# History product of a chunked recurrence: four heads side by side on TensorE, results through DRAM, no interleaving by hand

## The chip, the cores and the metric

The kernel runs on one core of a Trainium2 chip. The metric is the device time of one launch in microseconds; lower is better. The kernel before was timed three times: 3161.13, 3158.82 and 3152.03 us, median 3158.82 us.

## The reference, cut to what matters

The kernel is one decoder layer: a gated delta-rule attention, a long convolution and a mixture of experts, each followed by a layer norm. The change touches only the recurrence of the attention. For each of 16 sequences and 16 heads it is, over 128 time steps, with a state `S` of 128 x 128 in float32:

```
Sk = einsum('bhij,bhj->bhi', St, kt)
err = Sk - vt
Sn = at[..., None] * St - (bt[..., None] * err)[..., None] * kt[:, :, None, :]
ot = einsum('bhij,bhj->bhi', Sn, qt)
```

The state is never built. `S` at time t is a sum over earlier times r of a decayed vector u(r) times k(r), so `Sk` and `ot` are sums over r of u(r), scaled by the products k(r)·k(t) and k(r)·q(t), which an earlier stage put into a matrix `gram`.

## The kernel before, in words

`recurrence` puts 128 pairs (8 sequences x 16 heads) on the 128 partitions and calls that a group; there are two groups g. Time is cut into 8 chunks c of 16 steps. One (c, g) is a leaf, so there are 16 leaves, in the order (0,0), (0,1), (1,0) and so on. In the text below "round c" is a pair of leaves.

Inside a leaf VectorE walks the 16 steps (`leaf`, line 541 on). The second eight steps need sums over the first eight; part of them comes from TensorE: `cross_z` (line 771) for `Sk`, in five fills, and `cross_o` (line 797) for `ot`. Both multiply by diagonal matrices that ScalarE builds (`diagonal_z`, `diagonals_o`). VectorE adds the first fill of `cross_z` at line 627 at the start of the second half, and must have it there. TensorE may start `cross_z` of a leaf once VectorE has passed that leaf's first half (`half_done`) and `outputs` of the leaf before has read its bank (`o_seen`).

Everything older than the chunk is the history. At the end of leaf (c, g), for 0 < c < 7, VectorE multiplies all older rows in `hist[g]` by the chunk's decay, in pieces of 32 rows (line 664). SyncE stores the chunk's own 16 rows (lines 745 and 746) and then the decayed pieces (line 749) to `history` in DRAM, and loads them back turned, with the time rows on the partitions (line 762), beside the columns of `gram` (line 756). The turned rows of line 762 are loaded only when all stores have landed. One unit is four heads of one sequence; a leaf has 32 units in 8 buffers. For each head TensorE multiplies: stationary operand the turned rows (up to 112 x 128), moving operand 32 columns of `gram` (line 825). The result has the value index on the partitions. ScalarE copies it to `z_turn` (line 889), TensorE turns it back with 32 transposes per leaf (line 848), ScalarE copies those into `zo[g]` (line 915), and that is where leaf (c+1, g) starts from.

TensorE works in order. The units of the history product of leaf (c, g) are placed by hand with the table `ORDER`: some behind the last units of `cross_o` of the same leaf, 10 (rounds 0 to 2) or 8 (rounds 3 to 6) right behind `cross_o`, some between the units of `cross_z` of the following leaf, the rest behind it. GpSimd loads decays, `beta_v` and `gram` for later leaves and stores the outputs (`load_half`, `load_gram`, `store_o`).

Of the kernel before, what the change touches and what calls it, by code (L numbers as in the profile page):

```python
# [416 lines left out]
def recurrence(nc, a_dram, bv_dram, gram_dram, beta_dram, hist_dram, o_dram):  # L417
# [13 lines left out]
    HU = H // 4  # L431
    UB = H // HU
    UNITS = BG * UB
    NTURN = 8
# [9 lines left out]
    ORDER = ((0, 3, 12, 10, 4), (3, ROUNDS, 14, 8, 5))  # L444
    with ExitStack() as ctx:
# [14 lines left out]
        z_turn = m.sb("p2_z_turn", [DH, P, 2 * C])  # L460
        ident = m.sb("p2_ident", [P, P])
        NDZ, NDO = 2, 2
# [3 lines left out]
        ps_z = [m.ps(f"p2_ps_z{i}", [DH, H, 2 * C]) for i in range(2)]  # L466
        ps_t = [m.ps(f"p2_ps_t{i}", [P, 4, DH]) for i in range(2)]
# [33 lines left out]
        t_done = m.sem("p2_t_done")  # L501
        t_cp = m.sem("p2_t_cp")
        zo_ready = [m.sem(f"p2_zo_ready{g}") for g in range(GR)]
        TD = 2
        TB = 2 * C // 4
# [3 lines left out]
        with nc.Block() as start:  # L509
            @start.sync  # L510
            def _(sp):
                for sem in (*zo_ready, mm_done, z_cp, t_done, t_cp):
                    sp.sem_inc(sem, FREE)
                sp.sem_inc(diag_o_used, NDO)
# [22 lines left out]
        def _(dve):  # L537
# [3 lines left out]
            def leaf(c, g):  # L541
# [119 lines left out]
                if 0 < c < ROUNDS:  # L661
                    dve.wait_ge(kept[g], c * 2)
                    for r0, rows in pieces(c):
                        nc.vector.tensor_tensor(out=hist[g][:, r0:r0 + rows], in0=hist[g][:, r0:r0 + rows],
                                                in1=zo[g][:, 0, 0:1, :].broadcast_to([P, rows, DH]),
                                                op=ALU.mult).then_inc(hist_done[g], 1)
# [18 lines left out]
        def _(pool):  # L685
# [46 lines left out]
            for g in range(GR):  # L732
                pool.wait_ge(o_out[g], DMA * NCHUNK)


        @block.sync
        def _(sp):
            def by_seq(g, r0, n):
                return hist_dram[g, r0:r0 + n].rearrange("r p i -> p r i")

            for c in range(ROUNDS):
                rows, t1 = (c + 1) * C, (c + 1) * 2 * C
                for g in range(GR):
                    sp.wait_ge(leaf_done, c * GR + g + 1)
# [5 lines left out]
                    for u in range(UNITS):  # L750
                        n = g * UNITS + u
                        i = n % NTURN
                        b, h0 = u // UB, u % UB * HU
                        if c or n >= NTURN:
                            sp.wait_ge(mm_done, c * (GR * UNITS) + n - NTURN + 1 + FREE)
                        sp.dma_start(gcol[i][0:rows], gram_dram[g * BG + b, h0:h0 + HU, 0:rows, t1:t1 + 2 * C]
                                     .rearrange("h r e -> r h e")).then_inc(turned_in[i], DMA)
                        if u == 0:
                            sp.wait_ge(u_saved[g], (c + 1) * 2 * DMA)
                            if c:  # L760
                                sp.wait_ge(hist_saved[g], carried(c + 1) * DMA)
                        sp.dma_start(turned[i][0:rows], hist_dram[g, 0:rows, u * HU:(u + 1) * HU]).then_inc(turned_in[i], DMA)

        @block.tensor
        def _(pe):
            pe.wait_ge(cleared, 2 * NTURN + 2)

            def cross_z(c, g, between=lambda u: None):
# [6 lines left out]
                for j, (k0, k1) in enumerate(Z_FILLS):  # L775
                    if j == 4:
                        pe.wait_ge(x_z_read, c * (GR * len(Z_FILLS)) + g * len(Z_FILLS) + 1)
                    for k in range(k0, k1):
                        for q in range(2):
# [7 lines left out]
                            if not (k == k1 - 1 and q == 1):  # L787
                                between(u)
                    pe.wait_ge(diag_z_used, at + u)
                    pe.sem_inc(x_done, 1)  # L790
                    between(u)

            def cross_o(c, g, between=lambda u: None):
# [4 lines left out]
                for j, (k0, k1) in enumerate(O_FILLS):  # L798
                    for k in range(k0, k1):
                        for q in range(2):  # L800
# [7 lines left out]
                            between(u)  # L808
# [4 lines left out]
            for c0, c1, o_units, first, z_units in ORDER:  # L813
                with pe.Fori(c0, c1) as c:
                    for g in range(GR):
                        def history(u):

                            n = g * UNITS + u
                            i = n % NTURN
                            k = g * BG + u // UB  # L820
                            pe.wait_ge(turned_in[i], c * (GR * UNITS // NTURN * TD * DMA) + (n // NTURN + 1) * TD * DMA)

                            pe.wait_ge(z_cp, (c * (GR * BG) + k - 1 if k >= 2 else c * (GR * BG)) + FREE)
                            for h in range(HU):
                                last = nc.tensor.matmul(ps_z[k % 2][:, u % UB * HU + h, :], turned[i][:, h, :],  # L825
                                                        gcol[i][:, h, :], start=True, stop=True)
                            last.then_inc(mm_done, 1)

                        todo = list(range(UNITS))

                        def history_past(units):
                            def between(u):
                                if todo and u > units:
                                    history(todo.pop(0))
                            return between
# [19 lines left out]
        def _(act):  # L855
# [43 lines left out]
            for c in range(ROUNDS):  # L899
                rows_after = (2, 2, 2, 8, 12, 16, 16, 16) if c < 3 else (2, 2, 9, 13, 16, 16, 16, 16)  # L900
# [1070 lines left out]
```

## Time and profile before

| | us |
|---|---|
| median of three runs | 3158.82 |
| the profiled execution | 3169.36 |
| its span, first to last instruction | 3167.7 |
| first step of the recurrence on VectorE | 678.8 |
| last operation of the recurrence on VectorE ends | 2046.5 |
| VectorE busy, whole span | 2219.2 (70%) |
| TensorE matmuls busy, whole span | 2513.2 (79%) |
| mean granted TensorE clock | 0.821 of 2.4 GHz |

The recurrence takes 43% of the span. Times in rows are counted from the span's start. A busy share over the whole span mixes stages with different limits, so what a wait inside the recurrence costs has to be read inside it. TensorE has one record for the weight load (PEld) and one for the matmul (PE) of each pass; one float32 matmul of the kernel leaves two records of each.

### The profile page before, as it was taken

What the parts mean: (1) busy time and instruction counts of PE and PEld (TensorE: products, weight loads), DVE (VectorE), ACT (ScalarE), POOL (GpSimd) and SP (SyncE); (2) the same over time, 40 slices, a digit from 0 to 9 for tenths busy, and PEclk for the clock granted to TensorE, in tenths of its full rate; (3) what the DMA queues carried; (4) which work ended last, traced back from release to release, by engine and by line L of the source; (5) the groups of instructions that cost most, each with busy time, mean ns of one, the idle gap of its engine ahead of it and who ended that gap; (6) DMA issues with size and microseconds to landing.
All of it is one profiled execution on the core that took longest, in us unless ns stands there. A gap on an engine that the chain in (4) does not pass through costs nothing. (4 is left out here: it accounts for less than half of the span.)

```text
span 3167.7 us, 44608 instructions
## 1 busy us (share of the span) xinstructions
PE 2513.2 (79%) x12946; PEld 1944.7 (61%) x12946; DVE 2219.2 (70%) x5854; ACT 1250.0 (39%) x2980; POOL 773.2 (24%) x700
## 2 busy tenths in 40 slices
PE   8999999937989998989988888589968481389900
PEld 4555555526888888889887778478753250157700
DVE  5778778879888899898899987855527565013334
ACT  2555555524555555454555453532310010112200
POOL 1444344320000000000000000044435116501175
PEclk8999999967888888677877787899989665679955
DMA  2343434332233345655777775152230422029832
GB/s 95 119 125 118 123 121 122 118 110 69 73 84 92 106 130 137 160 148 149 193 206 203 209 190 152 37 163 73 76 107 20 133 98 74 6 83 267 245 100 87
DMA packets 488010, 389.69 MB, mean 123 GB/s; under 512 B 146255, under 2 KB 423550, under 8 KB 483336
## 3 DMA queue, kind: packets, MB, share of 16 engines
q1 hardware_dynamic: 440555, 285.62, 32.0%
q0 software_dynamic: 26784, 87.09, 9.0%
q10 hardware_dynamic: 20480, 14.69, 1.4%
q8 instruction: 89, 1.46, 0.2%
q14 instruction: 102, 0.84, 0.1%
HBM read 215.13 MB, written 178.41 MB: 124 GB/s over the span
## 5 line engine op out<-in xcount | busy, mean ns | idle before, releaser
L559 DVE SCALAR_TENSOR_TENSOR p_zo<-p_w,p_gd,p_zo 128x128 f32<-128x128 f32 x2304 | 649.0, 345 | 11.3
L825 PE MATMUL p_ps_z<-p_gcol,p_turned 112*128 112x32 f32 x3584 | 567.1, 322 | 55.9 <-DMA p_turned<-history 42.8
L825 PEld LDWEIGHTS p_ps_z<-p_gcol,p_turned 112*128 112x128 f32 x3584 | 560.8, 247 | 65.1 <-issue 37.4
L384 DVE SCALAR_TENSOR_TENSOR p_y<-p_ps_proj,p_w,p_y 128x508 f32<-128x508 f32 (+2 forms) x576 | 415.9, 741 | 114.0 <-ACT p_y L298 100.5
L804 PE MATMUL p_ps_x<-p_w,p_diag_o 128*128 128x128 f32 x2048 | 314.8, 305 | 69.0 <-ACT p_diag_o L866 45.5
L234 PE MATMUL p_ps_proj<-p_x,p_w 128*128 128x512 f32 x768 | 341.5, 594 | 2.7 <-ACT p_beta_t L289 2.7
L866 ACT ACTIVATE p_diag_o<-p_ident,p_gd 128x128 f32<-128x128 f32 x1024 | 316.7, 389 | 63.9 <-PE p_ps_x L804 55.2
L804 PEld LDWEIGHTS p_ps_x<-p_w,p_diag_o 128*128 128x128 f32 x2048 | 273.0, 209 | 106.3 <-ACT p_diag_o L866 65.1
L879 ACT ACTIVATE p_diag_z<-p_ident,p_gd 128x128 f32<-128x128 f32 x768 | 247.8, 390 | 212.4 <-PE p_ps_x L783 190.0
L783 PE MATMUL p_ps_x<-p_w,p_diag_z 128*128 128x128 f32 x1536 | 259.8, 317 | 61.2 <-DVEq L578 43.7
L783 PEld LDWEIGHTS p_ps_x<-p_w,p_diag_z 128*128 128x128 f32 x1536 | 221.3, 219 | 74.1 <-issue 50.9
L198 POOL TENSOR_TENSOR p_kq<-p_y,p_sig 128x512 f32<-128x512 f32 x128 | 162.5, 1274 | 376.3 <-ACT p_sig L309 375.7
L234 PEld LDWEIGHTS p_ps_proj<-p_x,p_w 128*128 128x128 f32 x768 | 141.6, 191 | 157.2 <-issue 153.9
L687 POOL DMA_DIRECT2D p_dec<-decays x32 | 17.3, 542 | 800.7 <-DVEq L660 738.7
L889 ACT COPY p_z_turn<-p_ps_z 128x512 f32<-128x512 f32 x112 | 64.7, 578 | 345.9 <-PE p_ps_z L825 345.9
L298 ACT ACTIVATE p_y<-p_ps_proj,p_w 128x512 f32<-128x512 f32 x192 | 149.3, 777 | 61.0 <-PE p_ps_proj L234 56.3
L556 DVE TENSOR_TENSOR p_w<-p_w,p_dec 128x256 f32<-128x256 f32 (+3 forms) x224 | 168.0, 750 | 0.5
L1086 PE MATMUL p_ps_g<-p_xT,p_wg 128*128 (+1 forms) x512 | 116.5, 387 | 33.8 <-DMA p_wg<-in_wgT 31.2
L256 PE MATMUL p_ps_gram<-p_kq 128*128 128x256 f32 x512 | 129.4, 396 | 4.6 <-POOL p_v L198 4.6
L1563 PE MATMUL p_ps_d<-p_sd,p_hs 88*128 88x256 f32 x128 | 58.7, 637 | 89.7 <-DVE p_hs L1685 49.2
L1086 PEld LDWEIGHTS p_ps_g<-p_xT,p_wg 128*128 128x128 f32 x512 | 98.3, 194 | 49.7 <-DMA p_wg<-in_wgT 31.4
L309 ACT ACTIVATE p_sig<-p_y 128x512 f32<-128x512 f32 x192 | 119.5, 623 | 4.5 <-issue 3.5
(213 smaller groups left out, 3600.3 us busy)
## 6 DMA issues: line engine op xcount, KB each, us to landing
history<-p_hist SPq DMA_DIRECT2D x18, 2048.0 KB, 10.8
gram<-p_gram SPq DMA_DIRECT2D x64, 512.0 KB, 3.3
p_wgu<-in_wguT SPq DMA_DIRECT2D x64, 352.0 KB
decays<-p_dec SPq DMA_DIRECT2D x64, 256.0 KB, 2.3
beta_v<-p_bv SPq DMA_DIRECT2D x64, 256.0 KB, 2.4
p_dec<-decays POOLq DMA_DIRECT2D x32, 512.0 KB, 6.4
p_w<-beta_v POOLq DMA_DIRECT2D x16, 1024.0 KB, 5.9
heads_out<-p_zo POOLq DMA_DIRECT2D x16, 1024.0 KB, 9.4
```

The lines of the kernel that those rows point to most:

```text
L198: nc.gpsimd.tensor_tensor(out=dst, in0=y[u % 4][:].rearrange("p (b t) -> p b t", b=QB), in1=sig[u % 2][:].rearrange("p (b t) -> p b t", b=QB),
L234: last = nc.tensor.matmul(ps_proj[u % 4][:], w_sb[j % 2][:, k, kind, :], x_sb[:, k, n * 512:(n + 1) * 512], start=(k == 0), stop=(k == KT ...
L298: nc.scalar.activation(y[u % 4][:], ps_proj[u % 4][:], ACT.Identity, bias=par[j % 2][:, kind, TAPS:TAPS + 1], scale=par[j % 2][:, kind, TA ...
L384: nc.vector.scalar_tensor_tensor(out=yv[:, :, s:], in0=pv[:, :, 0:T - s], scalar=par[j % 2][:, kind, TAPS - 1 - s:TAPS - s], in1=yv[:, :, ...
L556: return done(nc.vector.tensor_tensor(out=out, in0=in0, in1=in1, op=ALU.mult))
L559: return done(nc.vector.scalar_tensor_tensor(out=acc, in0=row, scalar=scalar, in1=acc, op0=ALU.mult, op1=ALU.add))
L783: last = nc.tensor.matmul(ps_x[:, j % 4, k - k0, :], diag_z[u % NDZ][:, e, :], w[g][:, 1 + r, :], start=(r == 0), stop=(r == RZ - 1))
L804: last = nc.tensor.matmul(ps_x[:, O_BANK + j, k - k0, :], diag_o[u % NDO][:, e, :], w[g][:, 1 + r, :], start=(r == 0), stop=(r == RO - 1))
L825: last = nc.tensor.matmul(ps_z[k % 2][:, u % UB * HU + h, :], turned[i][:, h, :], gcol[i][:, h, :], start=True, stop=True)
L866: last = nc.scalar.activation(diag_o[u % NDO][:, e, :], ident[:], ACT.Copy, scale=gd[g][:, r0 + e, C + HALF + k:C + HALF + k + 1])
L879: last = nc.scalar.activation(diag_z[u % NDZ][:, e, :], ident[:], ACT.Copy, scale=gd[g][:, r0 + e, HALF + k:HALF + k + 1])
L1086: last = nc.tensor.matmul(ps_g[g % 2][:, e, :], wg[:, k, (2 * g + e) * DH:(2 * g + e + 1) * DH], xT_sb[:, k, bass.ds(p * (PB * T), PB * T) ...
```

## The change

Stationary and moving operand change places. The stationary operand is now the 32 columns of `gram` of a head, the moving one its turned rows (128 columns), and four heads write to four groups of 32 partitions of one PSUM tile. The result has (head, column) on the partitions and the value index along the row. A unit is eight heads: 16 units per leaf, in 4 buffers of twice the size; the turned rows are loaded in pieces of 4 KB instead of 2 KB. `z_turn`, the 32 transposes and the copies of line 915 are gone. Instead ScalarE copies each sequence's result to `sums` and issues a DMA to a DRAM scratch `history_sums` (8 stores of 256 KB per leaf), and SyncE loads it into `zo[g]` in two halves of 1 MB.

`ORDER` and the interleaving are gone: TensorE does `cross_o`, then all 16 units, then `cross_z` of the following leaf. `gram` columns of the first four units are loaded ahead of the leaf's end. For those four units the chunk's own 16 rows are loaded once they have been stored, and the older rows once their stores have landed. Decay, store and load of the older rows stay at the end of the leaf. ScalarE has four buffers for `diag_z` instead of two: it makes four of the 16 `diag_z` units ahead of the eight copies of the history product, and twelve behind them.

```diff
-    HU = H // 4
+    HU = H // 2
-    NTURN = 8
+    NTURN = 4
+    QUADS = HU // 4
-    ORDER = ((0, 3, 12, 10, 4), (3, ROUNDS, 14, 8, 5))
+    NZ = 4
+    TL = 2 * (UNITS // NTURN) + 1
-        NDZ, NDO = 2, 2
+        NDZ, NDO = 4, 2
...
-                dve.wait_ge(zo_ready[g], c + FREE)
+                if c:
+                    dve.wait_ge(zo_in[g], c * (2 * DMA))
...
+            sp.wait_ge(cleared, 2 * NTURN + 2)
             for c in range(ROUNDS):
                 rows, t1 = (c + 1) * C, (c + 1) * 2 * C
+                known = c * C if c else HALF
...
+                    for u in range(NTURN):
+                        load_columns(u)
+                    sp.wait_ge(leaf_done, at + 1)
...
+                    sp.wait_ge(u_saved[g], (c + 1) * 2 * DMA)
+                    for u in range(NTURN):
+                        load_rows(u, known, rows)
+                    if c:
+                        sp.wait_ge(hist_saved[g], carried(c + 1) * DMA)
+                    for u in range(NTURN):
+                        load_rows(u, 0, known)
+                    for u in range(NTURN, UNITS):
+                        load_columns(u)
+                        load_rows(u, 0, rows)
+                    sp.wait_ge(o_out[g], (c + 1) * DMA)
+                    if c + 1 < ROUNDS:
+                        sp.wait_ge(kept[g], (c + 1) * 2)
+                    for half in range(2):
+                        seqs = slice(half * ZB * H, (half + 1) * ZB * H)
+                        for i in range(NS):
+                            sp.wait_ge(z_out[i], (at * 2 + half + 1) * DMA)
+                        sp.dma_start(zo[g][seqs].rearrange("p f s i -> p (f s) i"), sums_dram[g, seqs]).then_inc(zo_in[g], DMA)
...
+            with pe.Fori(0, ROUNDS) as c:
+                for g in range(GR):
+                    cross_o(c, g)
+                    for u in range(UNITS):
+                        k = g * BG + u // UB
+                        pe.wait_ge(turned_in[u % NTURN], c * (GR * TL * DMA) + (g * TL + 3 + 2 * (u // NTURN)) * DMA)
+                        pe.wait_ge(z_cp, c * (GR * BG) + k + 1)
+                        for q in range(QUADS):
+                            for h in range(4):
+                                last = nc.tensor.matmul(ps_z[k % NZ][h * 2 * C:(h + 1) * 2 * C, u % UB * QUADS + q, :],
+                                                        gcol[u % NTURN][:, q * 4 + h, :], turned[u % NTURN][:, q * 4 + h, :],
+                                                        start=True, stop=True)
+                        last.then_inc(mm_done, 1)
+                    cross_z(*following(c, g))
...
             def batch_row(c, g, b):
...
+                nc.scalar.copy(sums[b % NS][:], ps_z[b % NZ][:]).then_inc(z_cp, 1)
+                act.wait_ge(z_cp, k + 1 + NZ)
+                act.dma_start(sums_dram[g, b * H:(b + 1) * H].rearrange("(q h) e i -> (h e) q i", h=4),
+                              sums[b % NS][:]).then_inc(z_out[b % NS], DMA)
...
                     diagonals_o(c, g)
+                    for u in range(NDZ):
+                        diagonal_z(*following(c, g), u)
                     if c + 1 < ROUNDS:
                         keep(c, g)
+                    for b in range(BG):
+                        batch_row(c, g, b)
+                    for u in range(NDZ, DUNITS):
                         diagonal_z(*following(c, g), u)
```

## Rows read from the trace of the kernel before

**Rows 1.** What VectorE waited for, 670 to 2050 us: total, times, longest

```profile
DVE p_zo L627 <- PEq L790: 100.2, 47, 6.1
DVE p_w L563 <- ACTq L918: 14.3, 3, 7.7
DVE p_pp L673 <- PEq L810: 1.5, 1, 1.5
```

**Rows 2.** Groups by line: engine, operation, count | busy, mean ns | idle before, releaser

```profile
L825 PE MATMUL p_ps_z<-p_gcol,p_turned 112*128 112x32 f32 x3584 | 567.1, 322 | 55.9 <-DMA p_turned<-history 42.8 <-PE p_ps_x L783 13.0
...
L915 ACT COPY p_zo<-p_ps_t 128x512 f32<-128x512 f32 x112 | 65.1, 587 | 37.2 <-PE p_ps_t L848 35.3
```

**Rows 3.** Timeline, VectorE, leaf (7,1): start, duration, line, operation, count [idle before]

```profile
1972.15 0.22 DVE L600 COPY p_w<-p_dec 128x128 f32<-128x128 f32 x1
...
2010.82 0.29 DVE L627 TENSOR_TENSOR p_zo<-p_zo,p_ps_x 128x128 f32<-128x128 f32 x1
```

**Rows 4.** Timeline, VectorE, from the end of leaf (6,0) into leaf (6,1)

```profile
1770.86 13.09 DVE L664 TENSOR_TENSOR p_hist<-p_hist,p_zo 128x4096 f32<-128x4096 f32 x3
1784.13 0.22 DVE L600 COPY p_w<-p_dec 128x128 f32<-128x128 f32 x1
...
1828.78 0.29 DVE L627 TENSOR_TENSOR p_zo<-p_zo,p_ps_x 128x128 f32<-128x128 f32 x1 [6.08 <-PEq L790]
1831.93 0.29 DVE L627 TENSOR_TENSOR p_zo<-p_zo,p_ps_x 128x128 f32<-128x128 f32 x1 [2.23 <-PEq L790]
```

**Rows 5.** Timeline, SyncE: first store and first turned load behind leaves (0,0), (3,0), (6,0)

```profile
750.44 0.37 SPq L745 DMA_DIRECT2D history<-p_zo  x1
...
758.30 0.33 SPq L762 DMA_DIRECT2D p_turned<-history  x1
...
1244.74 0.38 SPq L745 DMA_DIRECT2D history<-p_zo  x1
...
1263.48 0.48 SPq L762 DMA_DIRECT2D p_turned<-history  x1
...
1770.80 0.38 SPq L745 DMA_DIRECT2D history<-p_zo  x1
...
1799.16 0.33 SPq L762 DMA_DIRECT2D p_turned<-history  x1
```

**Rows 6.** DMA issues, 1771 to 1868 us: count, KB each, median us to landing

```profile
p_turned<-history SPq DMA_DIRECT2D x32, 224.0 KB, 3.5
...
p_gcol<-gram SPq DMA_DIRECT2D x32, 56.0 KB, 3.1
p_dec<-decays POOLq DMA_DIRECT2D x2, 512.0 KB, 8.0
p_w<-beta_v POOLq DMA_DIRECT2D x1, 1024.0 KB, 8.6
heads_out<-p_zo POOLq DMA_DIRECT2D x1, 1024.0 KB, 10.5
...
p_gd<-gram POOLq DMA_DIRECT2D x1, 256.0 KB, 8.2
```

**Rows 7.** Stretches: us, busy time of each engine, granted clock, DMA share, GB/s

```profile
1775.00:1799.00 24.00, 17.05 (x100) 14.99 (x98) 23.83 (x55) 16.69 (x50) 0.00 (x0) 0.75 1.04 303
1799.00:1826.00 27.00, 19.89 (x131) 18.74 (x130) 22.95 (x64) 9.34 (x30) 3.96 (x5) 0.72 0.92 256
1840.00:1850.00 10.00, 9.62 (x86) 9.44 (x85) 8.96 (x33) 5.56 (x18) 0.00 (x0) 1.00 0.68 171
```

**Rows 8.** Timeline, TensorE: history units in round 0 and round 6

```profile
770.31 18.89 PEld L825 LDWEIGHTS p_ps_z<-p_gcol,p_turned 112*128 112x128 f32 x88
...
1805.34 0.97 PEld L825 LDWEIGHTS p_ps_z<-p_gcol,p_turned 112*128 112x128 f32 x8
1805.45 0.98 PE L825 MATMUL p_ps_z<-p_gcol,p_turned 112*128 112x32 f32 x8
```

**Rows 9.** Timeline, ScalarE, two units of `diag_z`, round 6

```profile
1805.48 1.85 ACT L879 ACTIVATE p_diag_z<-p_ident,p_gd 128x128 f32<-128x128 f32 x6
```

More of the change, by code:

```diff
@@ L459, in recurrence @@
         gcol = [m.sb(f"p2_gcol{i}", [C + OLD, HU, 2 * C]) for i in range(NTURN)]
-        z_turn = m.sb("p2_z_turn", [DH, P, 2 * C])
+        NS = 4
+        sums = [m.sb(f"p2_sums{i}", [P, UB * QUADS, DH]) for i in range(NS)]
         ident = m.sb("p2_ident", [P, P])
-        NDZ, NDO = 2, 2
+        NDZ, NDO = 4, 2
         DZ, DO = RZ // 2, RO // 2
@@ L500, in recurrence @@
         z_cp = m.sem("p2_z_cp")
[L501 to L505, printed above, removed]
+        z_out = [m.sem(f"p2_z_out{i}") for i in range(NS)]
+        zo_in = [m.sem(f"p2_zo_in{g}") for g in range(GR)]
+        ZB = BG // 2
         FREE = 1
@@ L661, in leaf, with decay_history @@
                 if 0 < c < ROUNDS:
[L662 to L666, printed above, removed]
+                    decay_history(c, g)
+            def decay_history(c, g):
+                dve.wait_ge(kept[g], c * 2)
+                for r0, rows in pieces(c):
+                    nc.vector.tensor_tensor(out=hist[g][:, r0:r0 + rows], in0=hist[g][:, r0:r0 + rows],
+                                            in1=zo[g][:, 0, 0:1, :].broadcast_to([P, rows, DH]),
+                                            op=ALU.mult).then_inc(hist_done[g], 1)
+                dve.wait_ge(hist_done[g], carried(c + 1))
             def outputs(at):
@@ L733, in _ @@
                 pool.wait_ge(o_out[g], DMA * NCHUNK)
+            for i in range(NS):
+                pool.wait_ge(z_out[i], GR * ROUNDS * 2 * DMA)
         @block.sync
@@ L766, in _, with cross_z @@
             pe.wait_ge(cleared, 2 * NTURN + 2)
-            def cross_z(c, g, between=lambda u: None):
+            def cross_z(c, g):
                 at = c * (GR * DUNITS) + g * DUNITS
@@ L812, in _ @@
             cross_z(0, 0)
[L813 to L835, printed above, removed]
-                        cross_o(c, g, history_past(o_units))
-                        for _ in range(min(first, len(todo))):
-                            history(todo.pop(0))
-                        cross_z(*following(c, g), history_past(z_units))
-                        for u in todo:
-                            history(u)
-                        pe.wait_ge(z_cp, c * (GR * BG) + (g + 1) * BG + FREE)
-                        for t in range(TB):
-                            k = g * TB + t
-                            pe.wait_ge(t_cp, (c * (GR * TB) + k - 1 if k >= 2 else c * (GR * TB)) + FREE)
-                            for e in range(4):
-                                last = nc.tensor.transpose(ps_t[t % 2][:, e, :], z_turn[:, :, t * 4 + e], ident[:])
-                            last.then_inc(t_done, 1)
```

67 lines of the change are left out of this document (23 added, 44 removed).

## The prediction

> **What bounds the kernel now.** I read the page's busy shares and slices first, then asked the trace only about the recurrence. It is a stage of its own, 1368 us of the 3167.7 (678.8 to 2046.5), and nothing outside it is edited. The waits of VectorE in it come next [rows 1]: together 116.0 us. So VectorE works in 92% of the stage, in one chain of small dependent operations, and the stage can only gain or lose by what VectorE waits for. The reader should see three kinds: 100.2 us for TensorE's `cross_z` (47 waits of at most 6.1 us), 14.3 us for the history sums at the start of a leaf, 1.5 us for `cross_o`. TensorE's 567 us in the history product and ScalarE's copies [rows 2] are off that chain, unless they make `cross_z` late. Then I took single leaves of the timeline. Leaf (7,1) has no history product ahead of its `cross_z`, and line 627 comes without a wait 38.7 us after the leaf's first step [rows 3]. That is VectorE's own pace, and with it I date the need of every leaf. In leaf (6,1) the same point comes 44.7 us after the first step, 6.08 of it waiting [rows 4]. Last, the queue of SyncE and the DMA rates [rows 5 to 7], because the product cannot start before its rows are back from DRAM.
>
> The change moves all 16 units of a product in front of the following `cross_z`. So the question of each leaf is: is the whole product done when VectorE wants its first fill?
>
> **What goes away.** If the product is early, `cross_z` stands alone on TensorE as in leaf (7,1), and both the 100.2 us and the 1.5 us go. The 14.3 us go in any case: the sums no longer wait for transposes and copies. They need a store and a load instead, and have most of a leaf for it. In round 6 the product ends about 77 us behind the leaf's end (below). Some 10 us more for a 256 KB store and 2 MB of loads gives 87. The leaf's successor in the same group starts a full leaf later: 13.3 us of decay, 72 us of steps (leaf (7,1), 1972.2 us to the end of the stage, less the two operations on outputs), and its own stall of some 28 us, so about 113. The reserve is some 25 us; without it the excess would be paid once per leaf. The 32 transposes of a leaf free TensorE and the eight copies behind them 4.7 us of ScalarE [rows 2], both off the chain: nothing.
>
> **When VectorE needs the first fill.** Counted from the first store behind a leaf's end: the decay, which takes 13.1 us for 96 rows in round 6 [rows 4], 2.2 us per round, and then 38.7 us. Need = 38.7 + 2.2c: 38.7, 40.9, 43.1, 45.3, 47.5, 49.7, 51.9 us for c = 0 to 6.
>
> **When the product is done.** First turned load of old rows behind the first store: 7.9 us in round 0, 18.7 in round 3, 28.4 in round 6 [rows 5]; between them I interpolate (11.5, 15.1, 21.9, 25.2). This is store time of the decayed rows, and the change keeps all of it.
> Then the loads. Old units are 224 KB of turned rows and 56 KB of `gram` columns, 32 of them in round 6 [rows 6]: 7.34 + 1.83 = 9.17 MB, times (c+1)/7 in other rounds. The columns fetched ahead are 8 old units' worth, 0.46 MB, in the same proportion. To be added, because it moves through the same engines in the same time: seven of the eight stores of sums, 1.84 MB; `beta_v` and `gram` for the next round, 1.31 MB; one half of the decays, 0.52 MB; the output store, 1.05 MB [rows 6]. The `beta_v` load today waits behind the last `cross_o` units and starts during the loads; now those units are done earlier, so it starts among the stores of history and delays them by what it takes off the loads. The sum is the same. Total in MB by round: 6.0, 7.2, 8.5, 9.7, 10.9, 12.2, 13.4.
> Rate: the stretch 1799 to 1826 us moves 256 GB/s at a DMA share of 0.92, so 278 GB/s when full [rows 7]. With four larger buffers and no TensorE work in between I take it as full. Landing of the last unit to the first fill: 1.5 us (the last unit and two `diag_z` units that are ready).
> Done = first load + MB / 0.278 + 1.5: 31, 38.9, 47.0, 55.1, 62.8, 70.5, 78.2 us. Against the need: rounds 0 and 1 early; late by 3.9, 9.8, 15.3, 20.8, 26.3 us in rounds 2 to 6. Sum 76, two leaves each: 152 us.
> Behind the first fill of these ten leaves: twelve `diag_z` units are made only after the last copy of sums, at 0.93 us each [rows 9]. The second and third fill wait about 2.5 us together (none in leaf (7,1), over 2.2 for the second alone in (6,1) [rows 4]; I take the middle because four units are ready ahead). 10 x 2.5 = 25 us.
>
> **TensorE's own time.** No row shows four 32-column operands side by side. Today one old unit, 8 records, takes 0.98 us with the granted clock at 2.4 GHz, and 88 records take 18.9 us in a stretch where it is 1.2 GHz (0.215 us each) [rows 8]. The upper bound for a new unit of 16 records is that pace without any overlap: 1.95 or 3.4 us; the lower bound is a quarter, 0.5 or 0.85 us. I take the lower: different columns of the array, different partitions of PSUM. At either 0.5, 0.85 or 1.95 us the DMA, at 2.1 us per new unit in round 6, is slower, so it matters in early rounds only. The Trainium skill (TensorE: Matmul & The Clock Gate, Part 3) gives 2.38x for three column tiles in place of my four times; that would put a unit near 1 us and leave my sum alone. The same part says that a weight load overlaps running matmuls only when the row group differs. Here all four operands use the same rows; but so do today's units, and their loads (0.97 us busy) and matmuls (0.98 us) fill one and the same microsecond [rows 8], so the trace disagrees. By that rule the units would be serial, the second rival.
>
> SyncE's queue: per leaf 16 pairs instead of 32, half the issues. The waits for `o_out` and the sums stand behind all loads; what is queued behind them (columns ahead, next leaf's stores) isn't due before the next leaf's end, over 25 us later. ScalarE gains eight DMA issues, about 0.4 us each, ahead of the twelve `diag_z`; in the 2.5.
>
> **Sum.** 152 + 25 = 177 us of new waits against 116.0 of old ones: +61 us. Against the profiled execution, 3169.4, that is 3230; it lay 10.5 us above the median of the runs, so I predict 3220.
>
> **The rivals.**
> *Loads get cheap: faster.* Rows of 4 KB could cost a DMA engine no more than rows of 2 KB. The stretch 1840 to 1850 is nearly pure loading: 1.71 MB, six old units, 0.68 x 10 us, so 1.14 us a unit [rows 7]. If the 448 short pieces of `gram` in it take 0.39 us, the turned rows take 0.75, and halving that saves 12 us in round 6 and in proportion elsewhere. The late times become 0, 2.9, 6.7, 10.5, 14.3; 69 us in two leaves, and 20 for the fills behind: 89 against 116, -27 us, 3132. It decides the sign from a saving of about 9 us in round 6. For it: stores at 303 GB/s and share 1.04 in 512-byte pieces [rows 7], so bytes aren't at their limit in the loads. Against: the `gram` pieces stay as short as they are, and they may be the larger half (303 GB/s at share 1.04 over 16 engines is 28 ns for a 512-byte piece; 448 pieces at that price are 0.79 of the 1.14 us), which saves only 5.6 us: +21, 3180.
> *The four operands don't overlap.* With the clock high: 31 us for 16 units from about 2 us after the first load. Done at 43, 46, 50 us in rounds 0 to 2, late by 4, 5.5, 7, and about 1.5 us more in the others: some +40 us more, 3258. With the clock low throughout, as in the 18.9 us row, 54.6 us: late by 25 to 36 in every leaf, about +350, 3510. For low: TensorE now idles between `cross_o` and the first unit, and today's 32-column stream ran at 1.2 GHz. Against: where `diag_z` matmuls, which move 128 columns, run between the units, the clock is at 2.4 GHz (1.00 in 1840 to 1850 us [rows 7]).
> *DMA is slower:* at the 256 GB/s as measured, +101, 3259; this belongs to the forecast's own range.
> *The product isn't late:* the next leaf starts from sums that come in time either way, so if loads and stores overlapped more than today, all 116 us would go, 3043. The DMA share of 0.92 to 1.04 in those stretches speaks against it [rows 7].
>
> **How the numbers follow.** Forecast (DMA-bound, +20 to +115 us): 0.64, own range 3178 to 3275. Cheap loads, ending faster: 0.15. Between them, within 0.3% (9.5 us, about what a measurement of this kernel can tell): 0.06. Serial operands, high clock: 0.11; low clock: 0.03. The last: 0.01. Faster 0.16, same 0.06, slower 0.78. The range 3132 to 3290 leaves out half of the cheap-load case and the upper tail.
>
> **What would show it.** VectorE's waits at line 627 should vanish in rounds 0 and 1 and grow from about 4 us in round 2 to 26 in round 6, almost all on the first fill; the waits at a leaf's start should be gone. The last turned load of round 6 should be issued some 70 us behind the leaf's end with the DMA share near 1 from the end of the leaf until then. A first-fill wait in rounds 0 and 1 would prove TensorE the bound; one under 15 us in round 6 would prove the loads cheaper than I count them, and my prediction wrong.

## The result, and the profile after

The changed kernel takes 3289.69 us (median of four runs, 3286.12 to 3291.72) against 3157.59: ratio 1.0419, 95% interval 1.0400 to 1.0438. It is slower by 132 us; 3220 was predicted, in a range up to 3290. Its profiled execution took 3291.08 us, 1.4 above its own median, while that of before (3169.36) lay 11.8 us above its median. From span to span it is 3289.5 - 3167.7 = 121.8 us. The recurrence's first step comes 3.6 us later (682.65 against 679.03 us), in code that the change doesn't touch. The other 118 us are in the recurrence, which ends at 2168.2 us in place of 2046.5.

VectorE's waits from 660 to 2200 us in the changed kernel, and the product's group with its reasons for idling (engine, operation, count | busy, mean ns | idle before, releaser). They answer to [rows 1] and [rows 2]:

```profile
DVE p_zo L628 <- PEq L818: 234.7, 42, 26.6
```

```profile
L848 PE MATMUL p_ps_z<-p_turned,p_gcol 112*32 112x128 f32 x3584 | 229.7, 415 | 587.6 <-DMA p_turned<-history 582.9 <-ACT p_sums L893 3.6
```

Line 628 is line 627 of before. 234.7 us stand there in place of 100.2, and the 14.3 and 1.5 us are gone: 234.7 - 116.0 = 118.7 us, which is the whole difference inside the stage. TensorE's product fell from 567 to 230 us of busy time, and TensorE now idles 583 us in it, for turned rows from DRAM. The change took work off an engine that wasn't the bound, and made a wait on the path longer.

The timeline of VectorE in the changed kernel, leaf (1,1), leaf (2,1) and leaf (6,1), each from its first step (line 601) to its first fill (in the last one, the first two), with the waits in brackets, against [rows 3, 4]:

```profile
908.51 0.22 DVE L601 COPY p_w<-p_dec 128x128 f32<-128x128 f32 x1
...
952.53 0.29 DVE L628 TENSOR_TENSOR p_zo<-p_zo,p_ps_x 128x128 f32<-128x128 f32 x1 [5.46 <-PEq L818]
...
1074.16 0.22 DVE L601 COPY p_w<-p_dec 128x128 f32<-128x128 f32 x1
...
1125.97 0.29 DVE L628 TENSOR_TENSOR p_zo<-p_zo,p_ps_x 128x128 f32<-128x128 f32 x1 [13.25 <-PEq L818]
...
1877.94 0.22 DVE L601 COPY p_w<-p_dec 128x128 f32<-128x128 f32 x1
...
1943.11 0.29 DVE L628 TENSOR_TENSOR p_zo<-p_zo,p_ps_x 128x128 f32<-128x128 f32 x1 [26.61 <-PEq L818]
1945.00 0.29 DVE L628 TENSOR_TENSOR p_zo<-p_zo,p_ps_x 128x128 f32<-128x128 f32 x1 [0.97 <-PEq L818]
```

(The trace names the fill by the leaf that waits; the rows that make it wait belong to the leaf before: (1,0), (2,0) and (6,0).) The wait on the first fill grows from 1 us behind round 0 to 26.6 behind round 6. SyncE in the same kernel shows what the product is waiting for, behind leaf (2,0) and leaf (6,0): first store, first store of old rows, and the eight loads for the first four units, against [rows 5]:

```profile
1069.37 0.38 SPq L770 DMA_DIRECT2D history<-p_zo  x1
...
1073.89 0.36 SPq L774 DMA_DIRECT2D history<-p_hist  x1
1074.81 17.56 SPq L764 DMA_DIRECT2D p_turned<-history  x8
...
1864.48 0.39 SPq L770 DMA_DIRECT2D history<-p_zo  x1
...
1868.99 18.03 SPq L774 DMA_DIRECT2D history<-p_hist  x3
1887.07 10.93 SPq L764 DMA_DIRECT2D p_turned<-history  x8
```

And the stretches in which TensorE works through the units, in rounds 0, 2, 3 and 6, against [rows 7]. The numbers are the length in us, the busy time of TensorE's matmuls, its weight loads, VectorE, ScalarE and GpSimd, then the granted clock, the DMA share and GB/s. The DMA share is the sum of the packets' times over the time of 16 DMA engines. It exceeds 1 in some stretches, so 1 isn't its ceiling.

```profile
768.00:790.00 22.00, 14.41 (x248) 10.32 (x252) 21.30 (x57) 4.10 (x7) 1.71 (x2) 0.58 0.73 204
1095.00:1123.00 28.00, 13.83 (x229) 8.47 (x221) 17.05 (x44) 4.10 (x7) 1.71 (x2) 0.56 1.04 239
1280.00:1308.00 28.00, 13.90 (x208) 7.84 (x208) 16.70 (x43) 4.04 (x7) 1.71 (x2) 0.50 1.06 266
1901.00:1940.00 39.00, 16.32 (x248) 9.02 (x240) 14.83 (x36) 4.10 (x7) 1.71 (x2) 0.50 1.11 293
```

The reader should see that round 0 has a DMA share of 0.73 only, and that from round 2 on, at a share above 1, the DMA still doesn't move at one rate: 239 GB/s in round 2, 293 in round 6. The same in whole, from the first store behind leaves (0,0), (2,0) and (6,0) to the end of the product:

```profile
753.50:790.80 37.30, 15.21 (x257) 10.72 (x257) 36.20 (x109) 6.05 (x9) 4.51 (x6) 0.55 0.75 208
1069.40:1123.00 53.60, 17.94 (x273) 12.11 (x273) 42.34 (x116) 10.74 (x26) 4.50 (x6) 0.59 0.93 233
1864.50:1940.20 75.70, 19.27 (x273) 11.29 (x271) 51.01 (x118) 8.40 (x22) 4.52 (x6) 0.54 1.05 289
```

### The profile page after: what moved, and what is told of

It reads as the page before. It is cut to its first block and busy times, and to the rows that moved or that the text cites. A ratio compares the mean times of both kernels' runs of the same rounds, so it can differ in the third digit from the quotient of the medians.

```text
span 3289.5 us, 43219 instructions
## 1 busy us (share of the span) xinstructions
PE 2091.0 (64%) x12498; PEld 1448.6 (44%) x12498; DVE 2218.7 (67%) x5854; ACT 1171.2 (36%) x2868; POOL 772.8 (23%) x692
## 5 line engine op out<-in xcount | busy, mean ns | idle before, releaser
L848 PE MATMUL p_ps_z<-p_turned,p_gcol 112*32 112x128 f32 x3584 | 229.7, 415 | 587.6 <-DMA p_turned<-history 582.9
L848 PEld LDWEIGHTS p_ps_z<-p_turned,p_gcol 112*32 112x32 f32 x3584 | 139.0, 159 | 674.7 <-issue 476.4
L831 PE MATMUL p_ps_x<-p_w,p_diag_o 128*128 128x128 f32 x2048 | 302.4, 296 | 56.5 <-ACT p_diag_o L869 26.5
L893 ACT COPY p_sums<-p_ps_z 128x512 f32<-128x512 f32 x112 | 65.7, 586 | 691.8 <-PE p_ps_z L848 691.8
L831 PEld LDWEIGHTS p_ps_x<-p_w,p_diag_o 128*128 128x128 f32 x2048 | 259.7, 200 | 99.2 <-ACT p_diag_o L869 66.9
L813 PE MATMUL p_ps_x<-p_w,p_diag_z 128*128 128x128 f32 x1536 | 221.2, 306 | 93.2 <-DVEq L579 43.1
L882 ACT ACTIVATE p_diag_z<-p_ident,p_gd 128x128 f32<-128x128 f32 x768 | 232.9, 388 | 99.9 <-PE p_ps_x L813 82.8
L813 PEld LDWEIGHTS p_ps_x<-p_w,p_diag_z 128*128 128x128 f32 x1536 | 205.0, 216 | 112.1 <-issue 85.4
L628 DVE TENSOR_TENSOR p_zo<-p_zo,p_ps_x 128x256 f32<-128x256 f32 (+1 forms) x80 | 29.0, 363 | 234.9 <-PEq L818 234.7
## 6 DMA issues: line engine op xcount, KB each, us to landing
history<-p_hist SPq DMA_DIRECT2D x18, 2048.0 KB, 15.3
```

The lines of the kernel that those rows point to most:

```text
L813: last = nc.tensor.matmul(ps_x[:, j % 4, k - k0, :], diag_z[u % NDZ][:, e, :], w[g][:, 1 + r, :], start=(r == 0), stop=(r == RZ - 1))
L831: last = nc.tensor.matmul(ps_x[:, O_BANK + j, k - k0, :], diag_o[u % NDO][:, e, :], w[g][:, 1 + r, :], start=(r == 0), stop=(r == RO - 1))
L848: last = nc.tensor.matmul(ps_z[k % NZ][h * 2 * C:(h + 1) * 2 * C, u % UB * QUADS + q, :], gcol[u % NTURN][:, q * 4 + h, :], turned[u % NTU ...
L882: last = nc.scalar.activation(diag_z[u % NDZ][:, e, :], ident[:], ACT.Copy, scale=gd[g][:, r0 + e, HALF + k:HALF + k + 1])
```

## The experiments

Three theories say what sets the end of the product, and with it the first fill. Theory A: the product stands ahead of `cross_z`, and its end is set by the bytes that are stored and loaded up to then. Theory B: in the low rounds the four buffers' round trips set it. Theory C: the early `beta_v` load among the stores of history is what costs. All kernels are the changed one with one edit, unless said otherwise. The "first unit" is the start of the product's first matmul, "product's end" the end of its last one, both counted from the first store behind the leaf's end. In the changed kernel the end is 37.3, 43.7, 53.6, 57.6, 63.2, 69.1 and 75.7 us behind leaves (0,0) to (6,0). z_first, six_buffers, beta_late and quarter_sums ran on a chip on which the kernel before takes 3094.70 us, beta_behind_out, woven and woven_beta on one where it takes 3096.95. On the second the changed kernel itself was run again:

> The changed kernel itself, as the reference of this group of runs, since chips differ: 1.04 times the kernel before, with the same waits as in its first trace (234.7 us at the fills of cross_z).

3217.61 us, 1.0385 (1.0367 to 1.0402), 234.1 us of waits at the fills; a single leaf waits up to 3.3 us more or less than in the first trace. The recurrence ends at 2167.7 us here and at 2168.2 in the first trace, while the spans are 3226.3 and 3289.5. So the chips differ behind the recurrence, and these runs are compared with 1.0385 and 3217.61.

**`cross_z` first** (z_first).

```diff
                     cross_o(c, g)
                     for u in range(UNITS):
+                        if u == 0:
+                            cross_z(*following(c, g))
...
-                    cross_z(*following(c, g))
```

(and on ScalarE all `diag_z` ahead of the copies of sums)

> TensorE does cross_o, then cross_z of the following leaf, then all 16 units of the product; ScalarE makes all 16 diag_z units before the first copy of sums. All else is the changed kernel. Theory P (the place of the product is the whole loss; the sums have a leaf of slack): all 234.7 us of waits at the fills of cross_z go, 0 to 20 us of waits come back at the start of late leaves; 3055 to 3080 us, so below the kernel before (3158). Rival Q (the product only moves its lateness to the start of the next leaf of the group, since the buffers of the units stay full until cross_z is done): the loads of 12 units start at about 66 us behind the leaf's end instead of 37, in rounds 3 to 6 the sums come 10 to 25 us late; 3130 to 3200 us.

3074.73 us, 0.9925 (0.9903 to 0.9947): 143 us less than the changed kernel, and 0.75% faster than the kernel before. VectorE's waits in the stage, 660 to 2215 us:

```profile
DVE p_w L563 <- DMA p_zo<-history_sums: 89.6, 14, 22.7
```

All 234 us at the fills are gone: the place of the product, with the copies of its sums, is the cause. But 89.6 us came back at the leaves' start, 3 to 8 us in nearly every leaf and 22.7 in the last. Theory P had the mechanism and underrated the rest (0 to 20 us). Q named it: the first unit now waits until 43 to 49 us, and the sums have no slack left. There is a second link that neither theory had. SyncE's queue is in order, and the loads of the sums of leaf (5,1), then the first `gram` columns for leaf (6,0)'s product, stand in it ahead of the stores behind leaf (6,0):

```profile
1739.32 13.10 DVE L668 TENSOR_TENSOR p_hist<-p_hist,p_zo 128x4096 f32<-128x4096 f32 x3
...
1732.87 14.96 SPq L792 DMA_DIRECT2D p_zo<-history_sums  x2
1747.88 7.06 SPq L760 DMA_DIRECT2D p_gcol<-gram  x4
1754.99 0.56 SPq L770 DMA_DIRECT2D history<-p_zo  x1
```

VectorE ends the leaf's steps and starts the decay at 1739.3, and the first store is issued at 1755.0, 15.7 us later. In the changed kernel that store comes as soon as the leaf ends. The last leaf waits longest, 22.7 us: the leaf ahead of it has no decay of 13.1 us at its end in which the sums could arrive.

**Six buffers** (six_buffers; two `diag_z` buffers for lack of space). The semaphore counts that follow from it are left out here.

```diff
-    NTURN = 4
+    NTURN = 6
-        NDZ, NDO = 4, 2
+        NDZ, NDO = 2, 2
```

> Six buffers of units instead of four (and two diag_z buffers instead of four, for space). Theory B (in rounds 0 to 3 the loads run in round trips: a buffer is refilled only after its unit is multiplied, issued and landed, and the DMA engines idle or wait in between): the first-fill waits of rounds 0 to 3 fall by the excess over my sum (9, 7, 8, 5 us a leaf), 30 to 55 us less than the changed kernel, 3235 to 3260. Theory A (bytes alone set the end of the product; only what moves in that time counts): within 6 us of the changed kernel, 3284 to 3298, as two diag_z buffers less cost up to 1 us a leaf.

3224.80 us, 1.0433 (1.0377 to 1.0490), 229.5 us at the fills: no difference from 1.0385 that the intervals show. The product's end moves by -0.5, -4.2 and -2.2 us behind leaves (0,0) to (2,0), and by under 0.5 behind (5,0) and (6,0). The waits at the first fills alone add up to 183 us in place of 199, so the two buffers are worth 16 us in all, 7 of them in round 1. Behind the first fill 11 us are added, where the two `diag_z` buffers are missing. Theory B is refuted as the main cause.

**`beta_v` behind the whole product** (beta_late).

```diff
                         pool.wait_ge(diag_o_used, (at + 1) * DUNITS + NDO)
+                        pool.wait_ge(mm_done, (at + 1) * UNITS + FREE)
                         load_gram(c + 1, g)
```

> The load of beta_v, gram and beta for the next round waits until the whole product of the leaf is done, so its 1.31 MB are outside the time that counts. Theory A (bytes): 4.7 us less in each of the 12 to 14 late leaves, the same in all rounds, 55 to 65 us less than the changed kernel, 3225 to 3235. Theory B (round trips bound rounds 0 to 3): the gain is smaller than 3 us a leaf in rounds 1 to 3 and 4.7 in rounds 4 to 6, 30 to 45 us less, 3245 to 3260. Theory C (its place among the stores lengthens every landing behind it): more than 5 us a leaf in rounds 0 to 3, over 70 us less.

3107.99 us, 1.0052 (1.0030 to 1.0074): 110 us less. Waits at the fills of this kernel, and the landing of the decayed rows behind leaf (2,0) there and in the changed kernel (count, KB, median us to landing):

```profile
DVE p_zo L628 <- PEq L819: 114.3, 30, 17.8
```

```profile
history<-p_hist SPq DMA_DIRECT2D x1, 2048.0 KB, 9.1
```

```profile
history<-p_hist SPq DMA_DIRECT2D x1, 2048.0 KB, 16.8
```

Twice what A expected, and it looked like C. But the edit did more than I had said: GpSimd's queue is in order, so behind the new wait stood half of the decays and the output store. 1.31 + 0.52 + 1.05 = 2.9 MB left the time that counts, 10.4 us at 278 GB/s; the product's end moved by 10.3 us in round 2, by 8.8 in round 6 (means of both leaves). That fits A with the bytes that really moved. The next run parts A and C.

**`beta_v` behind the output store** (beta_behind_out).

```diff
                     if at:
                         store_o(at - 1)
+                        load_gram(cp + 1, gp)      # with its three waits, for leaf at - 1
...
-                        load_gram(c + 1, g)
```

> Only the load of beta_v, gram and beta (1.31 MB) moves: GpSimd issues it behind the store of outputs, in the middle of the next leaf, instead of 8 us behind the leaf's end; decays and the output store stay where they are. When it waited for the whole product, GpSimd's queue held the decays and the output store back too, 2.9 MB in all, and the product ended 8.8 us earlier in round 6 and 10.3 us earlier in round 2. Theory A (bytes in the time that counts, at 278 GB/s): 4.7 us of the product's end if it lands behind the product, less where it still overlaps its last units (late rounds): 40 to 60 us less than the changed kernel. Theory C (what it costs is the delay of the stores of history, whose landing went from 9.1 to 16.8 us in round 2): it gets back nearly all of the first unit's 3 to 7 us in every round, also in late ones, and 70 to 100 us in all.

3201.60 us, 1.0333 (1.0315 to 1.0351), 212.2 us at the fills: 16 us less, below what either expected. First unit and product's end in us, changed kernel (second run of it) to this one: behind (0,0) 15.1 to 12.7 and 36.0 to 33.3; behind (1,0) 18.5 to 13.2 and 43.6 to 36.5; behind (3,0) 25.8 to 20.7, but 58.4 to 58.6; behind (6,0) 36.2 to 32.6, but 76.5 to 75.3. C is refuted from round 3 on: the stores land earlier, and the loads give it all back, because the same bytes meet them later. In rounds 0 and 1 the move does help: the load is issued 30 and 33 us behind the first store, when the last turned rows have been issued (27 and 31) and the product is within 4 us of its end.

**A quarter of the sums** (quarter_sums).

```diff
-                              sums[b % NS][:]).then_inc(z_out[b % NS], DMA)
+                              sums[b % NS][:, 0:1]).then_inc(z_out[b % NS], DMA)
-                        seqs = slice(half * ZB * H, (half + 1) * ZB * H)
+                        seqs = slice(half * ZB * H, half * ZB * H + 4)
```

> Left out: three quarters of each store of sums (64 KB instead of 256 KB) and nearly all of their loads, so the recurrence starts its leaves from stale sums. Theory A (bytes): 1.4 MB less in the time that counts, 5 us a leaf in 12 to 14 leaves, 60 to 70 us less than the changed kernel, 3220 to 3230. Theory B (round trips): the stores are short and fit in the gaps of rounds 0 to 3, so 5 us only in rounds 4 to 6, 30 to 40 us less, 3250 to 3260.

3192.80 us, 1.0326 (1.0273 to 1.0380): 25 us less, 205.2 us at the fills. The left-out stores were worth about 2 us a leaf, not 5 (product's end behind (6,0) 73.2 for 75.7, behind (6,1) 76.0 for 75.6). My price for them was too high, and neither theory had it. While TensorE works through the units behind leaves (2,0) and (6,0):

```profile
1076.60:1104.70 28.10, 15.81 (x257) 10.01 (x257) 20.32 (x54) 4.10 (x7) 1.71 (x2) 0.56 0.87 185
1870.40:1907.90 37.50, 17.31 (x257) 9.70 (x257) 15.66 (x39) 4.09 (x7) 1.71 (x2) 0.50 1.02 262
```

The rates fall with the bytes, from 239 and 293 GB/s to 185 and 262, and the time hardly does. So bytes alone don't set the product's end, least of all in the low rounds, where the DMA share is now 0.87.

**Half pieces** (two_kb). This run, no_old_store, old_all_ahead and woven_tuned ran where the kernel before takes 3157.91 us. The changed kernel wasn't run again with them; they are compared with its first result, 3289.69 us and 1.0419, beside which the kernel before took 3157.59.

```diff
+                        for f in range(2):
+                            sp.dma_start(turned[u % NTURN][r0:r1, f * 4:f * 4 + 4],
+                                         hist_dram[g, r0:r1, u * HU + f * 4:u * HU + f * 4 + 4])...
```

> Each load of turned rows is issued as two, of four heads each, so that its pieces are 2 KB as before the change. The predicted rival (4 KB pieces cost a DMA engine no more than 2 KB pieces) expects the loads 8 to 12 us longer in round 6 and less in proportion before, 70 to 100 us more than the changed kernel. Theory A (cost by bytes) expects 0 to 10 us more, from the issues alone.

3296.61 us, 1.0432 (1.0412 to 1.0453), 7 us from the changed kernel, with 248.9 us at the fills, 14 more. Behind leaf (6,0) the product ends at 76.3 us for 75.7, where the rival wanted 8 to 12 us more. The rival of the cheap 4 KB pieces is refuted: the turned rows cost no more in 2 KB pieces. Behind (0,0) the product ends at 42.2 us for 37.3, with twice the issues and the same bytes. There bytes alone don't set its end.

**No stores of old rows** (no_old_store).

```diff
-                        sp.dma_start(by_seq(g, r0, n), hist[g][:, r0:r0 + n]).then_inc(hist_saved[g], DMA)
...
-                        sp.wait_ge(hist_saved[g], carried(c + 1) * DMA)
```

> Left out: the stores of the decayed older rows and the wait for them, so the product reads older rows without their later decays. VectorE still decays them. Theory A (stores and loads are one sum of bytes ahead of cross_z): the product ends 6.3 MB earlier in round 6, 20 us, 3.4 us a round less before; the first fills are late by under 8 us in every leaf, and of 234 us of waits 40 to 80 stay: 0.975 to 0.99 of the kernel before. Rival (the loads with their 4 buffers bound the end, and would only start earlier to run slower): over 120 us of waits stay, above 1.0.

3153.45 us, 0.9995 (0.9973 to 1.0018), 101.5 us at the fills, 7.9 the longest. This kernel leaves out a part of the work. 133 us of waits go, 136 us of time. The product behind leaf (6,0) ends at 57.0 us for 75.7, 18.7 us earlier for 6.3 MB. The time and the waits lie between the two theories' numbers; that no first fill is over 8 us late is as A had it. The old rows' way to DRAM is over half of the lateness. What is left, 5 to 8 us at the first fill from round 2 on, is there without it.

**The old product in the new order** (old_all_ahead, an edit of the kernel before).

```diff
-    ORDER = ((0, 3, 12, 10, 4), (3, ROUNDS, 14, 8, 5))
+    ORDER = ((0, 3, 99, 32, 99), (3, ROUNDS, 99, 32, 99))
-                rows_after = ...
+                rows_after = (2,) * 8
```

> The kernel before with only its order changed: all 32 units of a product behind cross_o and ahead of cross_z, as the changed kernel has it, with the old operands, transposes and copies. It tells what the new operands are worth in this order. If TensorE's clock stays low in the long runs of 32-column matmuls (1.7 us a unit, 54 us a product behind a first unit at 10 to 31 us), the first fills are late by 25 to 35 us in every leaf and the time is 1.11 to 1.15 of the kernel before. If the clock is high (31 us a product), the fills are late by 5 to 20 us and it is 1.03 to 1.07. The changed kernel, whose product is bound by DMA, is at 1.039; theory A expects this one to be worse than that.

3601.09 us, 1.1406 (1.1381 to 1.1431), 463.9 us at the fills, 31 to 40 in every leaf. TensorE in its timeline behind leaf (0,0):

```profile
764.66 52.88 PE L825 MATMUL p_ps_z<-p_gcol,p_turned 112*128 112x32 f32 x247
817.35 2.91 PE L783 MATMUL p_ps_x<-p_w,p_diag_z 128*128 128x128 f32 x12
```

0.21 us a record without a gap, the price of the 1.2 GHz stretch [rows 8]; the granted clock is 0.50 here too. The low clock was the first of the two cases expected, and it came. The order alone costs 443 us with the old product. All the rest of the change (operands, results through DRAM, larger units, columns ahead, four `diag_z` buffers) is worth 3601 - 3290 = 311 us in this order. No run parts the operands from the rest.

**Woven** and **woven with `beta_v` behind the output store** (woven, woven_beta).

```diff
+    AHEAD = ((0, 2, 12), (2, 4, 8), (4, ROUNDS, 6))
-            with pe.Fori(0, ROUNDS) as c:
+            for c0, c1, ahead in AHEAD:
+              with pe.Fori(c0, c1) as c:
...
+                        if u == ahead:
+                            cross_z(*following(c, g))
```

> TensorE does 12 units ahead of cross_z in rounds 0 and 1, 8 in rounds 2 and 3, 6 in rounds 4 to 6, and the rest behind it; the copies of sums go the same way on ScalarE. Theory P (only the units that are late do harm ahead of cross_z; those that are there in time should go first): the waits at the fills are under 25 us in all, and the product ends 5 us or more before it does with cross_z first, so of the 89.6 us of waits at the leaf's start less than 50 stay: 0.96 to 0.985 of the kernel before. Rival: the product's end hangs on the DMA alone, the waits at the leaf's start stay at 70 to 90 us, and it equals cross_z first, 0.99.

> Both of the last two: woven, and the beta_v load behind the output store. Theory A: the stores of history land earlier and the product ends some 5 us earlier, which takes 5 us from each of up to 14 waits at the leaf's start: 0.95 to 0.97 of the kernel before. Rival: the load now meets the last units, the stores of sums and their loads, and gives back what it took: as woven, within 0.3%.

3049.46 us, 0.9850 (0.9825 to 0.9875), and 3011.57 us, 0.9717 (0.9701 to 0.9734). The waits of woven_beta at the fills and at the leaves' start:

```profile
DVE p_zo L629 <- PEq L820: 18.6, 6, 11.9
DVE p_w L564 <- DMA p_zo<-history_sums: 10.0, 1, 10.0
```

Woven has 42.3 and 10.1 us there. P holds for the start of the leaf (10.1 us in place of 89.6) and for the time, at the edge of its range; its waits at the fills are more than the 25 us expected, all but 1.1 behind rounds 5 and 6. The 1.3 MB that were worth 16 us in the changed kernel are worth 38 here by the medians. Woven's four runs lie between 3041.8 and 3056.3 us, and the two profiled executions differ by 23 us, with 24 us less of waits; so take 23 to 38. The gain is at the fills (42.3 to 18.6), not at the leaves' start where it was expected.

> woven_beta with 4 units ahead of cross_z in round 6 instead of 6. In woven_beta 18.6 us of waits at the fills and 10 us at one leaf's start are left, all behind round 5. Expected: the waits at the fills go, the one at the leaf's start stays or grows by a few us; 5 to 15 us below woven_beta, 0.967 to 0.971 of the kernel before.

3069.30 us, 0.9718 (0.9700 to 0.9737): the same ratio, where 5 to 15 us less were expected. The fills wait 0.9 us in all, and 16.0 us in place of 10.0 stand at the start of the last leaf. The traces have 12 us less of waits, but the times don't show it. SyncE's stores are late here as in z_first: VectorE starts the decay behind leaf (6,1) at 1769.5 us, and the first store is issued at 1780.0. These two are the fastest kernels of the study, 2.8% below the kernel before.

## Why the prediction was right or wrong

*The bound and the sign: right.* The product ahead of `cross_z` is late, VectorE waits for it, and nothing else in the stage lost time: 118.7 us of added waits are the stage's whole loss, and putting `cross_z` first removes all waits at the fills.

*What goes away: right.* Neither sums nor `cross_o` are waited for in the changed kernel.

*When VectorE needs the fill: right.* In z_first no fill waits, and behind every product the first fill comes 38.7 us after the first step, as in leaf (7,1) before.

*When the product is done: wrong in size.* This is the step that failed. Forecast of the first-fill wait behind rounds 2 to 6: 3.9, 9.8, 15.3, 20.8, 26.3 us, and none behind rounds 0 and 1. Measured (mean of the two leaves): 12.2, 14.8, 17.7, 22.5, 26.6, and 1.0 and 4.7 behind rounds 0 and 1. The sum over leaves is 199 us against 152. Two terms were mis-sized.

The first is the one rate for all rounds, "278 GB/s when full", taken from a stretch of round 6. By it the product should have ended at 29.5, 37.4, 45.5, 53.6, 61.3, 69.0 and 76.7 us in rounds 0 to 6. It ended at 37.2, 43.0, 52.8, 57.4, 62.6, 69.4 and 75.7 (means). The bytes weren't the fault: with the stores and one half of the decays ahead of them my terms make 7.6, 12.1 and 21.3 MB in rounds 0, 2 and 6, and the trace has 7.8, 12.5 and 21.9. The rates were: 208, 233 and 289 GB/s, at DMA shares of 0.75, 0.93 and 1.05. In round 0 the DMA wasn't full at all. In rounds 2 to 6 this term makes 23 us of the miss.

The second is the 1.5 us from the last unit to the first fill, which has no row behind it. It took 2.6 to 3.0 us in every leaf, 14 us of the miss in rounds 2 to 6. Most of it are the first fill's twelve matmul records, at the low clock. Behind leaf (6,0), the records of the first and the second fill, and two stretches with their clock:

```profile
1940.14 2.84 PE L813 MATMUL p_ps_x<-p_w,p_diag_z 128*128 128x128 f32 x12
1943.27 1.60 PE L813 MATMUL p_ps_x<-p_w,p_diag_z 128*128 128x128 f32 x12 [0.29 <-PE p_ps_x L813]
...
1940.30:1943.10 2.80, 2.68 (x12) 2.48 (x12) 0.00 (x0) 1.63 (x5) 0.00 (x0) 0.56 0.86 210
1943.10:1948.00 4.90, 4.45 (x36) 4.17 (x36) 2.74 (x11) 4.65 (x16) 0.00 (x0) 1.00 0.62 144
```

Both errors together make rounds 0 and 1 late, 11.5 us in all. That the forecast of round 6 matches is luck: its product ended 1 us sooner than forecast, and the longer tail made up for it.

Why less moves in low rounds stays open. The queues of SyncE (q1), ScalarE (q10) and GpSimd (q0) in the stretches 1095 to 1123 and 1901 to 1940 us (packets, MB, share of the 16 engines):

```profile
q1 hardware_dynamic: 5602, 3.51, 63.1%
q10 hardware_dynamic: 3168, 1.57, 22.3%
q0 software_dynamic: 416, 1.57, 17.9%
...
q1 hardware_dynamic: 12697, 8.24, 84.9%
q10 hardware_dynamic: 3168, 1.57, 14.3%
q0 software_dynamic: 416, 1.57, 11.0%
```

All three moved less per busy engine in round 2: 12.4, 15.7 and 19.6 GB/s against 15.6, 17.6 and 22.9. It isn't the short `gram` pieces: they stand to the turned rows as 56 to 224 KB in every round, and so are a larger part of the traffic in round 6. The number of buffers is worth 16 us over all leaves (six_buffers).

*The sign for TensorE: wrong.* I wrote that a first-fill wait in rounds 0 and 1 would prove TensorE the bound. The waits came, and TensorE isn't the bound: in 768 to 790 us its matmuls are busy for 14.4 of 22 us, and most of its idle time there is for turned rows.

*The `beta_v` load: the sum rule right, its condition missed.* I wrote that moving it among the stores leaves the sum unchanged. From round 3 on beta_behind_out shows just that. In rounds 0 and 1 it isn't so, by 3 to 5 and 7 to 8 us a leaf: issued behind the output store, the load misses nearly all of a short product, and issued among the stores it doesn't.

*Behind the first fill: the price right, the count too low.* 2.5 us in each of ten leaves were forecast; 35.7 us in 14 leaves came (234.7 - 199.0), 2.5 each. All of them wait, since even early rounds are late: 11 of the 58 us that the waits exceed the forecast by.

*The base.* I priced the change against the profiled execution and took 10.5 us off the sum. The changed kernel's own profile lies 1.4 us above its median, so this correction makes 9 us of the 70 us between 3220 and the result, the later start of the stage 3.6, and the waits 58.

*TensorE's own time: right.* I took 0.85 us for a unit of 16 records at the low clock. Four units in a stream take 3.42 us behind leaf (2,0) (last section), a unit by itself 1.08. The rival of serial operands is refuted by the same row, the cheap 4 KB pieces by two_kb. My argument against cheap pieces was wrong in its price, though: the packet records of the trace before, 1840 to 1850 us, have 12.8 ns for a 128-byte `gram` piece, not 28, so the `gram` pieces are the smaller part, as the rival had it. It fails at its other half: while TensorE works through the units behind leaf (6,0), a 4 KB piece takes 217 ns in the changed kernel and a 2 KB piece 100 in two_kb. The Trainium skill (TensorE: Matmul & The Clock Gate, Part 3) says that a weight load overlaps running matmuls only when the row group differs. The trace doesn't agree: with all four operands on the same rows, 64 weight loads and 64 matmuls start together and take 3.15 and 3.42 us.

*The range* ended at 3290, and the result of 3289.69 is at its edge. The large errors had one sign: a product later than forecast in six of seven rounds, a tail twice as long, and more leaves late. A count of bytes at a rate from the busiest round needs a range that reaches further up than down.

## What to carry to other kernels

When in-order work is put ahead of something that the critical engine needs, ask when its last input lands, not how long it computes. Put ahead only the units whose data are there in time, the others behind: here that split turned +4% into -1.5%, and with the `beta_v` load behind the output store into -2.8%. Price a transfer by where it stands: from round 3 on, 1.3 MB moved within the time that counts gained nothing, and from round 2 on 2.9 MB moved out of it gained 9 to 10 us a leaf. But try it: 1.4 MB of stores left out gained 2 us, not 5. And whatever stands behind a wait in an issuing queue waits too: it made beta_late move 2.9 MB in place of 1.3, and z_first store 15.7 us late.

## What the runs showed of the hardware

Float32 matmuls with 32 stationary columns each, written to four groups of 32 partitions, take 0.05 us a record where the old ones took 0.21. The timeline of TensorE behind leaf (2,0) of the changed kernel, at a granted clock of 0.52, so nearly all at the 1.2 GHz level:

```profile
1093.19 3.15 PEld L848 LDWEIGHTS p_ps_z<-p_turned,p_gcol 112*32 112x32 f32 x64 [21.52 <-issue]
1093.20 3.42 PE L848 MATMUL p_ps_z<-p_turned,p_gcol 112*32 112x128 f32 x64 [21.34 <-DMA p_turned<-history]
```

A weight load takes 3.15 / 64 = 0.049 us and a matmul 3.42 / 64 = 0.053, against 0.215 at the low clock before [rows 8]: 4.4 and 4.0 times, where I had taken 4. The Trainium skill (TensorE: Matmul & The Clock Gate, Part 3) gives 2.38 times for three column tiles; no run here has three. How much comes from the four groups and how much from loading 32 columns instead of 128 no run parts.

At a DMA share of 1.04 to 1.11 the DMA moved between 239 and 293 GB/s with the mix of transfers in one and the same loop, and 2 KB pieces of the turned rows were no slower than 4 KB ones. The granted clock was 0.50 through the whole product in round 6 (1901 to 1940 us), where the kernel before had 0.72 to 1.00 [rows 7]. Inside the product TensorE waits for turned rows between the units all the same. At the first fill behind it the clock costs 1.2 us: its twelve records took 2.84 us where the next twelve took 1.60 at full clock.
